# The norm's aggregation, its factor and the order of the turns around a small spectral product (one core, float32)

## The reference

```python
x = x + conv3x3(_gn(x))        # layer 0
x = x + scan(_gn(x))           # layer 1, a recurrence along the columns
x = x + spectral16(_gn(x))     # layer 2: the change lies in it
x = x + spectral_full(_gn(x))  # layer 3: a product at every frequency, + bias
```

## Time and profile before

| what | us |
|---|---|
| median of 3 runs | 573.09 (572.53 to 574.57) |
| the profiled execution: its time | 571.37 |
| its span in the trace | 569.6 |
| PE busy | 522.1 (92%) |
| DVE busy | 465.2 (82%) |
| ACT busy | 387.7 (68%) |
| POOL busy | 296.0 (52%) |

### The profile page before, as it was taken

One profiled execution on the slowest core, in us unless ns is written; L12 is line 12 of the kernel. 1 busy time (PEld: TensorE's weight loads), 2 busy tenths in 40 slices (PEclk: granted clock), 3 DMA queues, 4 the chain that ended last, 5 costly groups with the idle time before them and its releaser, 6 DMA issues.

```text
span 569.6 us, 28853 instructions
## 1 busy us (share of the span) xinstructions
PE 522.1 (92%) x11502; PEld 415.1 (73%) x11502; DVE 465.2 (82%) x1245; ACT 387.7 (68%) x814; POOL 296.0 (52%) x423
## 2 busy tenths in 40 slices
PE   2999999779999999999999999998989999999995
PEld 2333333467777777777777799997868898999995
DVE  7679885568989898989899879887877897487886
ACT  2545979867777777777777896676748998656541
POOL 7665665046666666666666520211558899522000
PEclk9999999989999999999999999999999999999999
DMA  6920000011111111111111310000308887103334
GB/s 197 412 34 0 2 2 5 1 43 40 41 42 37 46 37 42 41 38 45 37 44 39 121 41 2 1 0 2 96 25 256 264 286 251 51 1 150 148 146 151
DMA packets 26044, 45.82 MB, mean 80 GB/s; under 512 B 5632, under 2 KB 16128, under 8 KB 25104
## 3 DMA queue, kind: packets, MB, share of 16 engines
q1 hardware_dynamic: 24912, 44.98, 24.7%
q10 hardware_dynamic: 672, 0.15, 0.1%
q0 software_dynamic: 416, 0.07, 0.1%
HBM read 28.53 MB, written 8.39 MB: 65 GB/s over the span
## 4 chain that ended last, share of the span: by engine, by line
PE 43%; DVE 31%; issue 11%; ACT 6%; POOL 3%; DMA 3%; DVEq 2%; SPq 0%; ACTq 0%; POOLq 0%
PE psum L619 14%; PE psum L648 8%; DVE spec L1360 8%; PE psum L826 8%; DVE spec L1352 6%; DVE spec L1363 6%; PE psum L786 4%; DVE small L1245 3%; PE psum L932 3%; PE psum L747 2%; POOL work L360 2%; ACT work L302 2%; DVE spec L1355 2%; DMA image<-x_dram 1%; DVE image L1623 1%
## 5 line engine op out<-in xcount | busy, mean ns | idle before, releaser
L683 PE MATMUL psum<-spec,matrices 128*32 128x128 f32 x3024 | 109.3, 278 | 14.2 <-ACT spec L1049 7.3
L683 PEld LDWEIGHTS psum<-spec,matrices 128*32 128x32 f32 x3024 | 76.1, 110 | 46.5 <-ACT spec L1049 46.5
L690 PE MATMUL psum<-spec,matrices 128*32 128x128 f32 x3024 | 107.3, 274 | 1.3 <-DMA spec<-work 1.3
L531 POOL TENSOR_TENSOR spec<-spec 64x128 f32<-64x128 f32 x126 | 70.6, 560 | 71.9 <-DVE spec L1363 71.9
L690 PEld LDWEIGHTS psum<-spec,matrices 128*32 128x32 f32 x3024 | 85.5, 110 | 4.1 <-issue 4.0
L648 PE MATMUL psum<-spec,matrices 128*64 128x512 f32 x384 | 86.2, 606 | 1.0 <-ACT spec L983 1.0
L509 POOL TENSOR_SCALAR spec<-image,small 32x960 f32<-32x960 f32 (+1 forms) x48 | 55.6, 1159 | 34.1 <-PE psum L648 21.7
L826 PE MATMUL psum<-work 128*32 128x128 f32 x2368 | 68.9, 273 | 4.9 <-POOL work L360 2.7
L360 POOL COPY work<-work 32x768 f32<-32x768 f32 x74 | 62.2, 841 | 18.5 <-DVE work L1467 7.3
L826 PEld LDWEIGHTS psum<-work 128*32 128x32 f32 x2368 | 63.9, 110 | 9.3 <-issue 7.4
L525 POOL TENSOR_TENSOR image<-image,spec 128x128 f32 (+1 forms) x128 | 69.4, 542 | 0.0
(11 more groups left out here) (153 smaller groups left out, 819.3 us busy)
## 6 DMA issues: line engine op xcount, KB each, us to landing
work<-w_dram SPq DMA_DIRECT2D x66, 256.0 KB, 3.3
spec<-work SPq DMA_DIRECT2D x124, 64.0 KB, 1.9
image<-x_dram SPq DMA_DIRECT2D x3, 2048.0 KB, 12.7
out_dram<-image SPq DMA_DIRECT2D x3, 2048.0 KB, 7.3
image<-x_dram SPq DMA_DIRECT2D x4, 512.0 KB, 6.0
work<-w_dram SPq DMA_DIRECT2D x1, 2048.0 KB, 8.0
out_dram<-image SPq DMA_DIRECT2D x4, 512.0 KB, 3.8
kept<-const_dram SPq DMA_DIRECT2D x1, 192.0 KB, 5.1
```

Of the source, the lines that this page charges most:

```text
L531: nc.gpsimd.tensor_tensor(straddled(h, ROWS_01, 0), *of, ALU.subtract).then_inc(lower_ready[h], 1)
L683: last = mm(psum[QUARTERS[hm], 4 * h + g, 0:HB], sv[:, g, QUARTERS[hm]], moving[hm], start=starts, stop=True)
L690: last = mm(psum[q, 4 * h + g, 0:HB], sv[:, 3 + g, q], e, start=True, stop=stops)
```

## The change

The 16 aggregations move: image 0's ahead of the loop, and five in each pass of the loop (three behind statistic 5, one each behind 7 and 9), each set behind a tiny `memset`, with a copy of the ten results to `mv` at the pass's end. The statistics lie in a small buffer that each pass reuses. `over_h` of the last group issues 5 and then 4 products of the identity, read by nobody, ahead of its waits. `rstd` moves from SBUF to PSUM bank 3, so its reciprocal stands behind DVE's copy of that bank. ACT spreads chunk 1 ahead of last_spectrum(6). On PE turn(2) is moved ahead of sum_gain(0), and turn(3) ahead of L877.

```diff
@@ -765,16 +765,22 @@
                     last.then_inc(w_done, 1)
             def over_h(j, last_group=False):
+                if last_group:
+
+                    for n in (5, 4):
+                        for _ in range(n):
+                            mm(psum[:, 7, P:2 * P], cm["ident"], cm["ident"], start=True, stop=True)
+                        pe.wait_ge(w_act, j * 12 + 10)
                 pe.wait_ge(w_act, j * 12 + 12)
                 pe.wait_ge(w_dve, j * 12 + 12)
                 if last_group:
-                    pe.wait_ge(stat2, B + 2)
+                    pe.wait_ge(stat2, NG + 2)
                     mm(psum[:, 7, 0:2 * B], group_m, mv, start=True, stop=True).then_inc(sum2, 1)
                 for n in range(8):
                     if last_group:
                         if n == 7:
-                            pe.wait_ge(stat2, B + 3)
+                            pe.wait_ge(stat2, NG + 3)
                     else:
                         if n in BY_DVE:
                             pe.wait_ge(t_dve, j * 2 + (3 + BY_DVE.index(n)))
@@ -872,11 +878,11 @@
             small_product(2)
             turn(1)
             small_product(3)
+            turn(2)
             sum_gain(0)
+            turn(3)
             pe.wait_ge(stat3, 1)
             mm(psum[:, 5, 0:B], group_m, delta, start=True, stop=True).then_inc(sum3, 1)
-            turn(2)
-            turn(3)
             for c in range(1, 4):
                 sum_gain(c)
             pe.wait_ge(l2_added, 4)
@@ -1099,7 +1105,7 @@
                     move_by_w(j + 1)
                 else:
                     a(primed, eps_c, ACT.Sqrt).then_inc(table_in, 1)
-                    act.wait_ge(stat2, B + 5)
+                    act.wait_ge(stat2, NG + 5)
                     a(rstd_in[:, 0:B], var[:, 0:B], ACT.Sqrt, bias=eps_c).then_inc(dev2, 1)
                 for n in (0, 1, 2, 4) if last_group else (0, 1, 2, 4, 6, 8):
                     act.wait_ge(h_done, j * 9 + (n + 1))
@@ -1132,8 +1138,8 @@
             act.wait_ge(diag_zeroed, 2)
             spread_small(0)
+            spread_small(1)
             last_spectrum(6)
-            spread_small(1)
             last_spectrum(8)
             move_small(0)
             spread_small(2)
@@ -1378,7 +1384,7 @@
             dve.wait_ge(added[1], W)
 
-            n2 = [0]
+            n2 = [NG]
             def step2(ins):
                 n2[0] += 1
@@ -1391,14 +1397,11 @@
             g16 = gs.rearrange("p (b k) -> p b k", k=2)
             def mean_of_all():
-                dve.wait_ge(half2, 32)
-                for b in range(B):
-                    step2(v.bn_aggr(mv[:, 2 * b:2 * b + 2], bn[:, 12 * b:12 * b + 12]))
                 settle2()
                 step2(v.tensor_tensor(sq, m16[:, :, 0], m16[:, :, 0], ALU.mult))
                 settle2()
                 step2(v.tensor_tensor(m16[:, :, 1], m16[:, :, 1], sq, ALU.add))
-                assert n2[0] == B + 2
+                assert n2[0] == NG + 2
             def variance_of_all():
                 dve.wait_ge(sum2, 1)
@@ -1407,7 +1410,7 @@
                 step2(v.tensor_tensor(sq, g16[:, :, 0], g16[:, :, 0], ALU.mult))
                 settle2()
                 step2(v.tensor_tensor(var, g16[:, :, 1], sq, ALU.subtract))
-                assert n2[0] == B + 5
+                assert n2[0] == NG + 5
             def move_by_w(j):
                 for n in BY_DVE:
@@ -1422,15 +1425,26 @@
                 if not last_group:
                     move_by_w(j + 1)
                     for k in range(10):
-                        v.bn_stats(bn[:, ds(j * 60 + (12 + 6 * k), 6)],
+                        v.bn_stats(bn[:, 12 + 6 * k:18 + 6 * k],
                                    image[:, ds(j * 5120 + (1024 + 512 * k), 512)]).then_inc(half2, 1)
                         if k in (3, 5, 7):
                             dve.wait_ge(h_done, j * 9 + (k + 1))
                             to_spectrum(v.tensor_copy, j, k).then_inc(h_dve, 1)
-
+                        if k in (5, 7, 9):
+
+                            dve.wait_ge(half2, j * 10 + (3 + k))
+                            v.memset(carrier, 0.0).then_inc(aggregated, 1)
+                            for i in range(3) if k == 5 else (k // 2,):
+                                v.bn_aggr(five[:, 2 * i:2 * i + 2], bn[:, 12 + 12 * i:24 + 12 * i]).then_inc(aggregated, 1)
+                    dve.wait_ge(aggregated, j * 8 + 8)
+                    v.tensor_copy(mv[:, ds(j * 10 + 2, 10)], five).then_inc(stat2, 1)
+
+            five = bn[:, 72:82]
             move_by_w(0)
             for k in range(2):
                 v.bn_stats(bn[:, 6 * k:6 * k + 6], image[:, 512 * k:512 * k + 512]).then_inc(half2, 1)
+            dve.wait_ge(half2, 2)
+            v.bn_aggr(mv[:, 0:2], bn[:, 0:12]).then_inc(stat2, 1)
             with dve.Fori(0, NG - 1) as j:
                 forward(j)
             mean_of_all()
@@ -1438,7 +1452,6 @@
             variance_of_all()
             dve.wait_ge(dev2, 1)
-            step2(v.reciprocal(rstd, rstd_in))
             step2(v.tensor_scalar(shift, g16[:, :, 0], float(H * W), None, ALU.mult))
             def last_spectrum(n):
@@ -1447,13 +1460,17 @@
 
             last_spectrum(3)
+
+            dve.wait_ge(h_dve, 3 * (NG - 1) + 1)
+            rstd_small = psum[:, 3, 0:B]
+            step2(v.reciprocal(rstd_small, rstd_in))
             dve.wait_ge(h_act, 6 * (NG - 1) + 3)
             dve.wait_ge(h_dve, 3 * (NG - 1) + 1)
             settle2()
             dc = spec[0:C, 0:B]
             step2(v.tensor_tensor(dc, dc, shift[0:C, :], ALU.subtract))
             settle2()
-            assert n2[0] == B + 8
+            assert n2[0] == NG + 8
             def scale_small(c):
@@ -1462,10 +1479,10 @@
                     dve.wait_ge(l2_spread_pool, 2 * c - 2)
                 src = chunk(c).rearrange("p (t r b) -> p t r b", r=2, b=B)
                 dst = l2_scaled[c % 2].rearrange("p (t k b) -> p t k b", k=3, b=B)
-                v.tensor_tensor(dst[:, :, 1:3], src, rstd.unsqueeze(1).unsqueeze(1).broadcast_to([P, CHUNK_T, 2, B]),
+                v.tensor_tensor(dst[:, :, 1:3], src, rstd_small.unsqueeze(1).unsqueeze(1).broadcast_to([P, CHUNK_T, 2, B]),
                                 ALU.mult).then_inc(l2_scaled_ready, 1)
                 v.scalar_tensor_tensor(out=dst[:, :, 0], in0=src[:, :, 1], scalar=-1.0,
-                                       in1=rstd.unsqueeze(1).broadcast_to([P, CHUNK_T, B]),
+                                       in1=rstd_small.unsqueeze(1).broadcast_to([P, CHUNK_T, B]),
                                        op0=ALU.mult, op1=ALU.mult).then_inc(l2_scaled_ready, 1)
             scale_small(0)
```

More of the change, by code:

```diff
@@ L124, in program @@
         sq = sm(16)
-        mean, rstd, shift = sm(16), sm(16), sm(16)
+        mean, shift = sm(16), sm(16)
         energy = sm(16)
@@ L244, in program @@
         half2 = sem("half2")
-        stat2, sum2, dev2 = sem("stat2"), sem("sum2"), sem("dev2")
+        aggregated, stat2, sum2, dev2 = sem("aggregated"), sem("stat2"), sem("sum2"), sem("dev2")
         stat3, sum3, dev3 = sem("stat3"), sem("sum3"), sem("dev3")
```

## The result

The changed kernel takes 570.5 us (569.76 to 570.59, 5 runs) against 573.41 us (572.53 to 575.12, 5 runs) for the kernel before: a ratio of 0.9941 with a 95% interval of 0.9921 to 0.9961. It is 2.9 us faster, where 1.0 was forecast. As a time it stands at the lower end of the range of 570.5 to 573.7.

The account below looks back on a forecast made before the run. Between 385 and 421 us, TensorE's waits for VectorE, POOL and ScalarE, then its own work, were taken as bounds. Terms -0.3 +0.28 -0.55 -0.45 give -1.0 us: 572.1 from 573.09, range 570.5 to 573.7.

Parts of the forecast that it names:

- the nine products: In TensorE's 2.69 us gap after the last over_w: 2.16 us of work that costs nothing and wins nothing.
- The rival on the clock: The clock falls in the 2.69 us gap in most timed runs; products win 1.7 us more, giving 570.4; chance 0.08.
- The sign that was there: Whole program: the profiled 571.37 us lay 1.7 us below the median of 573.09; that difference was carried into the forecast.
- The aggregation: VectorE, end of the last loop pass before the twelve copies: 0.3 us won, bounds 0.3 lost to 0.8 won.
- The reciprocal: VectorE, behind the copy of bank 3, on the path to scale_small(0): 0.28 us lost, bounds 0.3 lost to 0.4 won.
- The factor in PSUM: Scalings and spreads feeding the small products: faster scaling_small(1) gives 1.0 us at turn(0), of which ScalarE's spreads leave 0.55.
- The small new wait ahead of small_product(2): On TensorE ahead of small_product(2): a new gap of about 0.3 us, ended by ScalarE, was expected.
- The turns: TensorE from small_product(3)'s end to the last sum_gain: 6.4 us becomes 5.95, so 0.45 won, bounds 0.25 and 1.0.
- The products' cost: Ahead of the group product: the 18 instructions end at 393.9, before it can start at 394.1, so they cost nothing.
- The stretch as a whole: From the last over_w to the mix, between 385 and 421 us: 1.0 us shorter, reaching the end of the program.
- The mix: Behind keep_warm: taken to keep its length; the prediction was called wrong if that changed.

Follow-up runs that it names:

- the later groups of runs: The changed kernel timed again, unedited, beside the kernel before: 571.04 against 574.89 us on the same chip, 570.69 against 575.35 us on another.
- the six traces: Six profiled executions of the kernel before, unchanged: over_h is slow in three, keep_warm in two, neither in two.
- the 574.19 us without a fall: One extra profiled execution of the kernel before, unchanged, with neither over_h nor keep_warm slow: 574.19 us.
- the four later traces: Four more profiled executions of the kernel before, unchanged: 574.19, 574.96, 576.80 and 575.36 us.

## Why the prediction was wrong

**The step that failed** is the one on the nine products: "They also win nothing in this profile: the granted clock is 1.00 in the gap itself." For that execution it is true. The sum puts them at nothing. But the forecast was for timed executions, and in these the products are the largest single part, 2.5 us alone and 1.6 us in the changed kernel. A fall behind the gap costs 1.67 us (8.88 against 7.21), one ahead of keep_warm 1.50 (5.34 against 3.84), and by their clocks more than half of its timed executions (77 of 110) have at least one. The rival on the clock named the mechanism, at a chance of 0.08. That its 570.4 meets the measured 570.5 so closely is partly luck: it took its 1.7 us from the scan's start, it counted one fall in most executions at one gap where there are two such gaps, and the same pair of kernels came out 3.9 and 4.7 us apart in the later groups of runs. The Trainium skill ("TensorE: Matmul & The Clock Gate", Part 1) says that the same kernel can differ from run to run in when the clock changes, and the six traces agree: gaps of 2.67 to 2.69 us with the fall and without.

**The sign that was there:** the profiled execution, 571.37 us, lay 1.2 us under the quickest of the three timed runs, and these were 2 us apart. I carried that 1.7 us over as a constant. At least a part of it was falls that this execution didn't have, and a change can remove those: the changed kernel's profiled execution (570.59) is the slowest of its five timed ones, which are 0.8 us apart. Another part was scatter at other places, as the 574.19 us without a fall show, so one can't say that the 1.7 us was the clock alone.

**The aggregation** was forecast at 0.3 and gave 0.85: 0.45 at the group product, as the copies show (2.97 against 3.41 us after over_w), and 0.4 because the gap behind the copy of bank 3 vanished with it. That gap is in every trace of a kernel that keeps the 16 aggregations and in none of one that has them in the loop. Why is open; no row names a releaser that fits it. No pass of the loop became longer: from the start of the forward FFT to the last over_w it is 57.08 us, and was 57.10.

**The reciprocal** was forecast at 0.28 and costs 0.35. That the path as a whole is no longer is the aggregation's doing.

**The factor in PSUM** did what was forecast: L1482 and L1484 take 0.69 and 0.41 us, POOL's spreads 0.90 at most, and small_product(1) follows at once. Together with the reciprocal and ScalarE's order it gives 0.32, forecast 0.27. The small new wait ahead of small_product(2), ended by ScalarE, is there:

```profile
408.22 1.69 PEld L832 LDWEIGHTS psum<-work 128*32 128x32 f32 x64 [0.35 <-ACT work L360]
```

**The turns** were forecast at 0.45, and as a whole the traces show nothing. The last sum no longer waits for gain(3), as forecast, and less the pauses the new order is worth 0.42. But TensorE loses 0.24 to 0.78 us in turn(2), a pause that my sum had no term for. The working had a slip too: its terms (two turns at 0.87, 1.05, 0.13, three sums at 0.96, 0.2) add up to 6.0 us and not 5.95, which leaves 0.37 to win.

**The products' cost** was forecast at nothing. They end 0.2 us ahead of the group product, and yet it starts 0.15 us later after the last copy than without them (0.26 us behind it, and 0.11 before).

**The stretch as a whole** was forecast 1.0 us shorter. The parts, each read from its own trace, give 0.85 + 0.32 + 0.42 - 0.15 = 1.44, and 36.83 less the 35.37 without pauses is 1.46. The 1.22 of the profiled execution is near the forecast because the aggregation's extra 0.55 stood against the pause and the products' cost.

**The mix** doesn't keep its length. From its first product to the backward FFT the three executions of the changed kernel take 69.8, 69.1 and 69.8 us, other variants 69.5 to 72.1. With scatter of this size the timed differences of single parts (0.9, 0.9 and 0.4, each known to some 0.3) don't contradict what the stretch itself shows (0.85, 0.32 and 0, or 0.42 less the pauses), and the stretch is the better measure. Whether the parts also change the mix isn't shown; one trace of each variant is too few.

## What to carry to other kernels

A profile is one execution. Where timed runs scatter by more than a few tenths of a per cent, or the profiled one lies outside them, take more traces of the kernel before and compare the granted clock and the length of a fixed group of products in each, before costing an edit that fills an idle gap of TensorE at nothing.

Part the gain of several small edits by distances between marks within one trace, not by total times: stages that the edits don't touch scatter by more than the edits give.

Filling a gap pays where dense products follow it. At the scan's start, where other engines set the pace, 6.8 us at half clock cost only about 0.8 us.

## What was not expected of the hardware

- With idle gaps of the same length (2.67 to 2.69 us) TensorE's clock fell to its lower level in three of six executions of one program, and at a 1.73 us gap in two of six. With nine products in the first gap, neither fell in ten traces. At these two places a stay at the lower level lasted 3.4 us, and 6.8 us in one trace (over_h at 9.96 us).
- TensorE paused for up to 0.9 us within runs of small products whose inputs were all there. It did so in the middle of turn(2) in each of the three executions of the changed kernel, and earlier in the code, in small_product(3), where 30 more instructions stood ahead. The kernel before does it too: its first and second of the four later traces have 0.34 and 0.18 us in small_product(2), the one with the nine products alone 0.27. The traces with the aggregations behind the loop and with the turns behind the sums have none. Transfers of weights were under way at that time. That this is the supply of instructions is a guess; it wasn't tried.
- A pause of 0.5 us on VectorE, between a copy and a small operation whose inputs were ready, was there in all traces with the 16 aggregations behind the loop and in none with them inside.
